# A transformer layer on one core: the output projection of tiles 2 to 15 in pairs, by Strassen's seven block products

## What is computed

```python
xn = layernorm(x)
q, k, v = xn @ Wq, xn @ Wk, xn @ Wv           # 16 heads of 64; rotary embedding on q and k
att = softmax(causal(q k^T) / 8) @ v          # per batch and head
s = att @ Wo                                  # the output projection, 2048x1024 @ 1024x1024
g = silu(ffn(xn))                             # sign(weight), routed scales, bias
out = x + s * g
```

## Time and profile before

| What | Value |
|---|---|
| Median of three runs | 1168.62 us |
| The profiled execution, its own time | 1168.28 us |
| Its span, first to last instruction | 1166.5 us |
| Time outside the span | 1.78 us |
| PE busy | 1134.9 us, 97% of the span |
| DVE, ACT, POOL busy | 62%, 52%, 36% of the span |
| Granted TensorE clock, mean | 0.994 |

### The profile page before, as it was taken

One profiled execution on the slowest core, in us unless ns is written; L12 is line 12 of the kernel. 1 busy time (PEld: TensorE's weight loads), 2 busy tenths in 40 slices (PEclk: granted clock), 3 DMA queues, 4 the chain that ended last, 5 costly groups with the idle time before them and its releaser, 6 DMA issues.

```text
span 1166.5 us, 17720 instructions
## 1 busy us (share of the span) xinstructions
PE 1134.9 (97%) x5692; PEld 946.1 (81%) x5692; DVE 723.2 (62%) x1731; ACT 611.2 (52%) x1286; POOL 421.8 (36%) x254
## 2 busy tenths in 40 slices
PE   5899999999999999999999999999999999999998
PEld 3677767788888888888888888888888887888886
DVE  6756542477767777677776777767767678324222
ACT  6545543266655666556665566655666577412211
POOL 0434537343343433424334243342523434222120
PEclk9899999999999999999999999999999999999999
DMA  9425132210202202022360220202202034564753
GB/s 373 187 90 235 50 96 102 80 56 18 63 9 72 61 11 63 9 72 63 144 216 9 72 63 9 63 9 72 63 9 63 9 106 174 171 206 153 216 187 119
DMA packets 87271, 112.01 MB, mean 96 GB/s; under 512 B 3408, under 2 KB 68944, under 8 KB 86224
## 3 DMA queue, kind: packets, MB, share of 16 engines
q1 hardware_dynamic: 87248, 111.72, 28.9%
HBM read 78.15 MB, written 33.55 MB: 96 GB/s over the span
## 4 chain that ended last, share of the span: by engine, by line
PE 88%; DVE 5%; ACT 3%; POOL 1%; issue 1%; DMA 1%; SPq 0%; DVEq 0%; ACTq 0%; POOLq 0%
PE at_proj L44 17%; PE at_proj L46 17%; PE at_proj L45 17%; PE at_out L975 7%; PE ff_z_ps L287 6%; PE at_pt L962 6%; PE at_score L944 3%; PE at_score L945 3%; PE at_score L46 2%; PE at_score L45 2%; PE at_score L44 2%; POOL ff_xs_lo L676 1%; PE at_proj L929 1%; DVE xs_full L598 1%; ACT ff_xs_hi L419 1%
## 5 line engine op out<-in xcount | busy, mean ns | idle before, releaser
L44 PE MATMUL at_proj<-xn_hi,w_hi 128*128 128x512 f32 x896 | 361.9, 404 | 1.6 <-POOL w_lo L1400 0.8
L46 PE MATMUL at_proj<-xn_hi,w_lo 128*128 128x512 f32 x896 | 351.2, 392 | 0.0
L45 PE MATMUL at_proj<-xn_lo,w_hi 128*128 128x512 f32 x896 | 349.6, 390 | 0.0
L46 PEld LDWEIGHTS at_proj<-xn_hi,w_lo 128*128 128x128 f32 x896 | 168.3, 188 | 37.0
L44 PEld LDWEIGHTS at_proj<-xn_hi,w_hi 128*128 128x128 f32 x896 | 168.7, 188 | 31.8 <-issue 1.2
L45 PEld LDWEIGHTS at_proj<-xn_lo,w_hi 128*128 128x128 f32 x896 | 169.0, 189 | 30.3
L1384 POOL TENSOR_TENSOR at_turning<-at_turning,rope_table 128x512 f32<-128x512 f32 x64 | 82.9, 1296 | 289.3 <-DVE at_turning L1228 289.3
L1392 POOL TENSOR_TENSOR w_lo<-w_stage,w_hi 128x1024 fp32r<-128x1024 f32 x45 | 114.5, 2559 | 162.8 <-ACT w_hi L1060 162.8
L1098 ACT ACTIVATE at_prob<-at_score,at_neg_max 128x512 f32<-128x512 f32 (+3 forms) x256 | 133.3, 526 | 71.2 <-DVE at_neg_max L1256 70.8
L1107 ACT ACTIVATE at_pt_hi<-at_pt 128x512 fp32r<-128x512 f32 (+1 forms) x192 | 93.9, 524 | 99.9 <-PE at_pt L962 99.2
L1273 DVE TENSOR_TENSOR at_pt_lo<-at_pt,at_pt_hi 128x512 fp32r<-128x512 f32 (+1 forms) x192 | 112.0, 597 | 42.2 <-ACT at_pt_hi L1107 41.2
(11 more groups left out here) (125 smaller groups left out, 1824.4 us busy)
## 6 DMA issues: line engine op xcount, KB each, us to landing
z_store<-z SPq DMA_DIRECT2D x16, 512.0 KB, 2.9
w_stage<-in_L_attn_Wq_dram SPq DMA_DIRECT2D x16, 512.0 KB, 3.8
w_stage<-in_L_attn_Wk_dram SPq DMA_DIRECT2D x16, 512.0 KB, 5.1
w_stage<-in_L_attn_Wv_dram SPq DMA_DIRECT2D x16, 512.0 KB, 6.2
att_store<-at_att_t SPq DMA_DIRECT2D x32, 256.0 KB, 2.0
rope_table<-att_store SPq DMA_DIRECT2D x16, 512.0 KB, 6.6
z<-_attn_hidden_states_dram SPq DMA_DIRECT2D x16, 512.0 KB, 4.8
at_turning<-z_store SPq DMA_DIRECT2D x16, 512.0 KB, 6.1
```

The source lines that it names most:

```text
L44: pe.matmul(out, sh, mh, start=first, stop=False)
L45: pe.matmul(out, sh, ml, start=False, stop=False)
L46: return pe.matmul(out, sl, mh, start=False, stop=final)
```

## The change

Tiles 0 and 1 are projected as before. Tiles 2 to 15 are taken in seven rounds of two tiles. A round is a product of a 2x2 block matrix (two tiles by two halves of the inner dimension) with another (two halves of the inner dimension by two halves of the output columns). Eight block products are replaced by seven, by Strassen's scheme in Winograd's form. A block product is 4 blocks of the inner dimension times 3, which is 12 matmuls. Call a round's seven products P0 to P6, in PE's order; they use the operands A11, A12, S2, S1, S3, S4, A22 in that order. S1 to S4 are sums and differences of the attention blocks. The weights of P2, P3, P4 and P6 are T2, T1, T3, T4, sums and differences of blocks of Wo.

Per round the following is new. P0, P2, P4 and P6 all accumulate into one PSUM bank (a), P1 into a second (b), P3 and P5 into a third (c). Since partial results of bank a are needed on the way, ACT copies bank a after P0 and after P2 and bank c after P3 (`part_copy`, semaphore `partial_ok`); P2, P4 and P5 wait for these copies. P6 waits until DVE has read bank a after P4 (`block_read`). DVE makes the four sums of the attention rows (`row_sums`), the low parts of the four (`op_low`), and three blocks of the output with three instructions each (`block_out`) and one with two (`block_21`). ACT makes seven high parts (`op_hi`), POOL the low parts of A11, A12 and A22.

Once, ahead of round 0, Wo is loaded a second time, in four pieces of two 512 KB rows (`load_rows`), and T1 to T4 are made for each piece: four DVE additions (`sums`), four ACT copies (`sums_high`), two low parts on DVE and two on POOL (`sums_low`). The result is now added into x's own buffer and stored from there, so the load of x for tile n+2 waits for the store of tile n to land (`y_out`).

The core of the diff:

```diff
+            def load_z(n):
                 if n >= 2:
                     sp.wait_ge(y_add, n - 1)
+                sp.dma_start(z_tile[:, n % 2, :], z_store[tile_rows(n), :]).then_inc(xz_in[n % 2], 16)
+            def load_x(n):
+                if n >= 2:
+                    sp.wait_ge(y_out[n % 2], 16 * (n // 2))
                 sp.dma_start(x_tile[:, n % 2, :], io["x"][tile_rows(n), :]).then_inc(xz_in[n % 2], 16)
...
+            store_y(0)
+            load_z(2)
+            load_rows(3)
+            load_x(2)
+            store_y(1)
+            load_z(3)
+            for n in range(PLAIN, TILES, 2):
+                more = n + 2 < TILES
+                if more:
                     load_att(n + 2)
+                    load_att(n + 3)
+                load_x(n + 1)
+                store_y(n)
+                if more:
+                    load_z(n + 2)
+                    load_x(n + 2)
+                store_y(n + 1)
+                if more:
+                    load_z(n + 3)
...
+                product(a, A11, wo_block(0, 0), True)
+                pe.wait_ge(op_low_pool, 3 * q + 2)
+                product(b, A12, wo_block(1, 0), True)
+                pe.wait_ge(op_low_dve, 4 * q + 1)
+                pe.wait_ge(sum_low_dve, 2 * QT - 1)
+                pe.wait_ge(partial_ok, 3 * q + 1)
+                product(a, S2, wo_sum_block(T2), False)
+                pe.wait_ge(op_low_dve, 4 * q + 2)
+                pe.wait_ge(sum_low_dve, 2 * QT)
+                product(c, S1, wo_sum_block(T1), True)
+                pe.wait_ge(op_low_dve, 4 * q + 3)
+                pe.wait_ge(sum_low_pool, 2 * QT - 1)
+                pe.wait_ge(partial_ok, 3 * q + 2)
+                product(a, S3, wo_sum_block(T3), False)
+                pe.wait_ge(op_low_dve, 4 * q + 4)
+                pe.wait_ge(partial_ok, 3 * q + 3)
+                product(c, S4, wo_block(1, 1), False)
+                pe.wait_ge(op_low_pool, 3 * q + 3)
+                pe.wait_ge(sum_low_pool, 2 * QT)
+                pe.wait_ge(block_read, 3 * q + 2)
+                product(a, A22, wo_sum_block(T4), False)
...
+            for q in range(ROUNDS_W):
+                n = PLAIN + 2 * q
+                more = q + 1 < ROUNDS_W
+                part_copy(q, 0)
+                silu(n, 0)
+                silu(n + 1, 1)
+                part_copy(q, 1)
+                if more:
+                    op_hi(q + 1, A11)
+                    op_hi(q + 1, A12)
+                    op_hi(q + 1, S2)
+                part_copy(q, 2)
+                if more:
+                    for op in (S1, S3, S4, A22):
+                        op_hi(q + 1, op)
...
+            sums(0)
+            sums_low(0)
             gate(0, 0)
+            sums(1)
+            sums_low(1)
+            sums(2)
+            sums_low(2)
+            sums(3)
+            sums_low(3)
+            row_sums(0)
+            op_low(0, S2)
             gate(1, 1)
...
+            for q in range(ROUNDS_W):
+                more = q + 1 < ROUNDS_W
+                block_out(q, 0, 0, 0, False)
+                if more:
+                    row_sums(q + 1)
+                    op_low(q + 1, S2)
+                    op_low(q + 1, S1)
+                block_out(q, 2, 1, 1, False)
+                if more:
+                    op_low(q + 1, S3)
+                block_out(q, 1, 0, 1, True)
+                if more:
+                    op_low(q + 1, S4)
+                block_21(q)
```

More of the change, by code:

```diff
@@ L755, in attention_block @@
+        sum_b = sb("at_sum_b", [P, 2, EMBED], F32)
+        wo_sum = [[sb(f"at_wo_sum{t}_{part}", [P, QT, HALF], F32R) for part in ("hi", "lo")] for t in range(4)]
+        a22 = sb("at_a22", [P, 2, HALF], F32R)
+        partial = sb("at_partial", [P, 3, HALF], F32)
         wo_raw = keep["w_stage"]
@@ L760, in attention_block @@
         z_tile = turning[:].rearrange("p a b n -> p a (b n)")
-        y_tile = [prob[p][:, 0:EMBED] for p in range(2)]
+        wo_rows = [sum_b, keep["w_stage"][:, 0:2, :]]
+        att_sum = sum_b[:].rearrange("p a (b n) -> p (a b) n", b=2)
         proj_ps = [psum(f"at_proj{i}", [P, SEQ]) for i in range(2)]
@@ L796, in attention_block, with operand, att_rows, flat @@
         TILES = BATCH * QT
+        PLAIN = 2
+        ROUNDS_W = (TILES - PLAIN) // 2
+        A11, A12, S2, S1, S3, S4, A22 = range(7)
+        T1, T2, T3, T4 = range(4)
+        SUM_ORDER = (S1, S3, S2, S4)
+        def operand(op):
+            if op == A22:
+                return [a22[:, part, :].rearrange("p (k n) -> p k n", k=QT) for part in range(2)]
+            pair, half = ((2, 0), (2, 1), (0, 0), (0, 1), (1, 0), (1, 1))[op]
+            return [w[pair][:, QT * half:QT * (half + 1), :] for w in (w_hi, w_lo)]
+        def att_rows(op):
+            tile, half = {A11: (0, 0), A12: (0, 1), A22: (1, 1)}[op]
+            return att_raw[:, tile, half * HALF:(half + 1) * HALF]
+        def flat(ap):
+            return ap.rearrange("p k n -> p (k n)")
         def wait_wo(engine, k):
@@ L1047, in output_tile, with wo_block, wo_sum_block @@
                     output(n, p, o, range(KT))
-            with pe.Fori(1, TILES // 2) as i:
-                for p in range(2):
-                    output_tile(2 * i + p, p)
+            def wo_block(k_half, o):
+                cols = slice(o * HALF, (o + 1) * HALF)
+                return [[wo_part[QT * k_half + k][part][:, cols] for k in range(QT)] for part in (PHI, PLO)]
+            def wo_sum_block(t):
+                return [[wo_sum[t][part][:, k, :] for k in range(QT)] for part in (PHI, PLO)]
@@ new lines, in product, with strassen @@
+            def product(out, op, moving, first):
+                (sh, sl), (mh, ml) = operand(op), moving
+                for k in range(QT):
+                    last = split_matmuls(pe, out[:], (sh[:, k, :], sl[:, k, :]), (mh[k], ml[k]), first=(first and k == 0),
+                                         final=(k == QT - 1), reopened=not first)
+                last.then_inc(product_done, 1)
+            def strassen(q):
+                a, b, c = banks[q % 2]
+                if q == 0:
+                    pe.wait_ge(merged, 2 * STEPS)
+                elif q == 1:
+                    pe.wait_ge(y_mul, 2 * PLAIN)
+                else:
+                    pe.wait_ge(block_read, 3 * (q - 1))
+                    pe.wait_ge(block_a, q - 1)
+                pe.wait_ge(op_low_pool, 3 * q + 1)
+                product(a, A11, wo_block(0, 0), True)
[19 more added lines that the diff above has]
+                product(a, A22, wo_sum_block(T4), False)
@@ L1214, in _, with part_copy @@
+            def part_copy(q, which):
+                act.wait_ge(product_done, 7 * q + (1, 3, 4)[which])
+                if q >= 1:
+                    act.wait_ge(block_done, 3 * (q - 1) + (1, 3, 2)[which])
+                act.activation(partial[:, which, :], banks[q % 2][(0, 0, 2)[which]][:], ACT.Copy).then_inc(partial_ok, 1)
             silu(0, 0)
             silu(1, 1)
[L1216 to L1219, removed]
+            op_hi(0, A11)
```

214 lines of the change are left out of this document (172 added, 42 removed).

## The result

The changed kernel takes 1223.15 us (median of four, 1221.44 to 1224.56) against 1169.23 for the kernel before: a ratio of 1.0459, 95% interval 1.0446 to 1.0472. It is slower by 54 us, where 1216 us was forecast (range 1192 to 1230). The profiled execution took 1221.44.

A forecast was written before the change was run, and what follows sets the result against it. PE, 97% busy, bounds the old kernel; afterwards instruction order does. Round 0's y at 1055.8, five 26.5 us periods to 1188.3, last x 1200.0, products to 1210.0, end: span 1214.5, plus 1.8 outside: about 1216 us (1192 to 1230).

The forecast's parts named there:

- What is removed: Fewer matmuls on PE save 19.0 us over seven rounds; shorter DVE work at the very end saves 1.2.
- The start: Round 0's P2 waits for weight sums until 1033.8, the middle of 1030.3 and 1037.3; PE stands for 20 us.
- the lower end: P2 of round 0 at 1030.3, from adding up the instructions listed ahead of it in order.
- the upper end: P2 of round 0 at 1037.3, from letting DVE and POOL alternate.
- Round 0: x of tile 3 lands at X = 1044.6, five transfers behind a store; P4 starts at X + 1.75.
- X = y + 15.25: Second tile's x lands (X) eight transfers after the round's first tile is added (y): 15.25 us, 14.7 to 16.0.
- y = X + 11.25: From x landed to the next round's first addition: SiLU, copy, P4, P5, three DVE instructions, 11.25 us (9.3 to 12.5).
- the sum (1216.3): Whole kernel: start, five periods of 26.5 us, last round and end give span 1214.5, plus 1.8 outside it.
- The short end of a round: Lower limit of a round's length, given as 23.9 us beside the expected 26.5 and upper 28.5.
- Piece 0, gate(0,0) and pieces 1 and 2: DVE work at the start, from 998.9 on, claimed to last to about 1017.7.
- the copy is never late: Rival, 6%: y to X at most 9.6 us, rounds of 19.04 us, total 1168, 1164 at its lower end.
- What binds is who stands behind whom: In later rounds DVE, ACT and POOL have room; instruction order sets the 26.5 us round, against 19.04 without waits.

The follow-up runs named there:

- e13: e9 with results in a buffer of their own and the start's instructions reordered on SyncE, ACT, POOL and DVE: 1161.91 us, 0.9946 of the kernel before.
- e4: Changed kernel without the second Wo load and the weight sums with their splits, plain Wo blocks instead (output differs): 1201.3 us, ratio 1.0268 to the kernel before.
- e11: Changed kernel with the result written to and stored from a buffer of its own, so x needn't wait for that store: 1218.38 us, ratio 1.0422.
- e5: Changed kernel loading only 8 of 128 rows of z from tile 4 on (output differs): 1211.85 us, ratio 1.0366 to the kernel before.
- e2: Changed kernel with x of the second tile loaded ahead of the next round's attention rows on SyncE: 1225.51 us, ratio 1.0477 to the kernel before.
- e8: Changed kernel, three orders at once: ACT's copies before the second SiLU, x before attention rows, DVE's outputs before next row sums: 1174.69 us, ratio 1.0044.
- e7: Changed kernel with ACT's copies for P4 and P5 ahead of the second SiLU and the next round's operands: 1208.98 us, ratio 1.0345.
- e9: e8 with tiles 2 and 3 also projected plainly, six rounds, weight pieces spread behind tiles 0 to 3: 1163.87 us, 0.9954 of the kernel before.
- e3: Changed kernel with 20 useless matmuls into a free bank between P3 and P4 on PE: 1214.88 us, ratio 1.0380 to the kernel before.

## Why the prediction was right, and where it was off

- **What is removed: 19.0 and 1.2.** Right, by the four terms above and by those of `e13`; at the end it was 1.1.
- **The start: P2 at 1033.8 (1030.3 to 1037.3).** It came at 1035.23, 0.85 of it from before the stage. The middle was a choice between two ends, and that it fitted within 1.4 us is partly luck. What lay between them was DVE beside POOL. Four additions of weights and two of rows took 1.63 to 1.77 us instead of 0.69, 6.1 us more in all, of which 4.1 show at P2 (1035.2 less 0.85, against the 30.3 of the lower end). Where the engines met, they did alternate: each of these ends 0.55 us behind the POOL instruction that had begun before it. So strict alternation was the right rule, and why the upper end, worked out by it, lies 2.9 us behind the measured start is not shown:

```profile
1007.70 2.27 POOL L1719 TENSOR_TENSOR w_lo<-rope_table,w_hi 128x512 fp32r<-128x512 f32 x1
1008.74 1.77 DVE L1533 TENSOR_TENSOR w_stage<-w_stage 128x512 f32<-128x512 f32 x1
1010.54 0.69 DVE L1535 TENSOR_TENSOR w_stage<-w_stage 128x512 f32<-128x512 f32 x1
```

`e4` shows the price: 20.4 us for the sums.
- **Round 0: X at 1044.6, P4 at X + 1.75.** 1045.88 and X + 1.69.
- **X = y + 15.25.** 14.8, 15.8, 14.9, 15.4, 14.9; mean 15.2, and 11.9 in round 6 where 11.75 was worked out. The size was right. The reason, eight transfers at 1.75 each, holds by `e11`, but was half of it: the chain over the store's landing (13.0) stood right beneath. The model without it had `e5` gain twice what it did on x, and put x of `e2` at 11.8 instead of 12.5; that `e2` gained nothing at all is the work of P5's wait. The Trainium skill ("DMA: Bandwidth & Descriptors", anatomy of one DMA) has 436 GB/s behind a fixed 2.0 us, as a fit to DMAs that GpSimd issues, while SyncE issues these. The 316 GB/s here at a share of 1.01 do not agree with it; by an estimate from the page's figures x would have landed some 3.5 us earlier.
- **y = X + 11.25.** 11.2 in round 0, then 12.05, 11.75, 12.1, 12.0 and 12.2. The term mis-sized is P4 at the lower clock: 4.6 charged, 5.0 to 5.3 measured in rounds 1 to 5 (mean 5.2), since ten to twelve of its matmuls started 0.43 or more apart. A round so took 27.2 instead of 26.5. These 0.7 a round in five rounds, 1.3 at the first y and 0.4 behind the last round's y make the 5.1 us that the profiled execution (1221.4) is above the sum (1216.3). The other 1.7 is that execution against its median.
- **Slips in the sums.** The 0.3 by which the profiled execution lies below its median was named and not added: 1216.6. The short end of a round is 14.7 + 9.3 = 24.0, not 23.9. Piece 0, gate(0,0) and pieces 1 and 2 add up to 1015.6, not 1017.7, but P2 rests on piece 3. None of them moves the forecast by more than 0.3 us.
- **The rival "the copy is never late"** was rightly held unlikely. `e8` shows that the order alone decided this: the transfers fit into 19.4 us a round once nothing needed stands behind an instruction that waits for them. "What binds is who stands behind whom" was right, but applied only to ACT; `e7` showed DVE, and `e2` SyncE, in the same part.

Not tried: letting the SiLU wait for z alone and only the addition for x. What decides how soon behind a gap the lower clock comes stays open.

## What to carry to other kernels

Fewer matmuls are worth something only if the chain of small steps between products is off PE's path: before removing an eighth of a stage's matmuls, write down for each engine what stands in its list between the transfer that lands last and the instruction PE needs, on all engines at once, because moving one shows the next. A loop in which a transfer waits for a result and that result for the transfer repeats its full length each round, however idle the engines are; look for stretches in which the DMA engines stand idle while PE works on what releases the next transfers. Work done once "behind" something needs the idle time of every engine that it uses: here four pieces of 4.7 us each stood on DVE in the 15 us up to P2. Giving up one pair's saving of 2.7 us took the first wait from 20.5 to 8.8 (`e9`), and another order of the start took it to 4.2 (`e13`).

## What was not expected of the hardware

- A gap of PE costs more than itself, and not by its length alone. Behind 5.09 us (changed kernel) and 2.75 us (`e2`) the matmuls were 0.43 apart from the second on, eleven of them in the former, 2.5 us in all, and five in the latter. Behind 3.81 in round 0 of the changed kernel, 3.30 in `e5` and 3.44 in `e7` the first two to six still started at most 0.31 apart and the following seven 0.43. Behind 3.04 in `e2`, 2.59 in `e7` and 1.71 in `e5` none did, but behind 2.24 in `e3` seven did.
- In the last stage of the changed kernel 19 DVE instructions, 512 wide and with both inputs in SBUF, took 1.51 to 1.82 us instead of 0.69. Each began while a POOL instruction was running and ended 0.55 us behind that one's end; the 1024-wide one of the earlier trace rows took 3.29 instead of 1.23. DVE instructions that began ahead of the POOL one, or read PSUM, took 0.67 to 0.69 beside it.
- SyncE's issues take longer when several transfers are on their way: two issues of attention rows took 2.77 us behind three to four that had not landed (changed kernel), and one of x 3.18 behind five (`e11`), against 0.33 for x behind one.
